# Writing out eight turns instead of one of the expert-tile loop in a mixture-of-experts stage, with the runtime-tested loop kept for what may follow

## The reference

```python
h = tok_ref(x, w1, b1, w2, b2)             # four groups mixed by softmax weights of a small MLP
h = h + attn_ref(layernorm(h), ...)        # 16 heads of 16, causal within an image
h = h + ffn_ref(layernorm(h), ...)         # shared expert and 64 routed ones, width 128
...
scores = sigmoid(logits) + gate_bias       # best 4 of 8 groups, then the best 6 experts of a token
h = silu(einsum('th,eih->eti', x, eg_w)) * einsum('th,eih->eti', x, eu_w)
routed = einsum('eti,ehi,te->th', h, ed_w, comb)
```

## Time and profile before

| what | us |
|---|---|
| median of 3 runs (lowest, highest) | 588.38 (584.45, 591.64) |
| the profiled execution's own time | 591.47 |
| its span, first to last instruction | 589.6 |
| PE busy in the span | 489.3 |
| DVE, ACT, POOL busy | 338.3, 282.3, 250.4 |

### The profile page before, as it was taken

How to read it: one execution, slowest core, us unless ns; L and a number is a source line. 1 busy time by engine, 2 the same in 40 slices (tenths; PEclk the granted TensorE clock), 3 DMA queues, 4 the chain that set the end, 5 groups by cost and what they waited for, 6 DMA issues and landing times.

```text
span 589.6 us, 12682 instructions
## 1 busy us (share of the span) xinstructions
PE 489.3 (83%) x3000; PEld 363.8 (62%) x3029; DVE 338.3 (57%) x1077; ACT 282.3 (48%) x920; POOL 250.4 (42%) x279
## 2 busy tenths in 40 slices
PE   1779898897989898767469878999998899797996
PEld 1656676675767676444148756777777687573554
DVE  4754488788888787787534333443443243332697
ACT  3394877786667676652014333444444344341100
POOL 1120115555555555567704544564564464544000
PEclk9996999999999899997679999998999899997998
DMA  8999901111111111112235467466566646542896
GB/s 277 351 321 299 252 2 55 54 56 55 56 55 55 56 55 56 54 55 99 108 100 179 127 196 220 145 198 185 152 219 189 195 125 179 164 157 80 356 387 255
DMA packets 57591, 91.05 MB, mean 154 GB/s; under 512 B 7911, under 2 KB 44650, under 8 KB 57552
## 3 DMA queue, kind: packets, MB, share of 16 engines
q1 hardware_dynamic: 44880, 62.41, 34.9%
q0 software_dynamic: 10368, 26.07, 12.3%
q10 hardware_dynamic: 2304, 2.10, 1.0%
HBM read 87.09 MB, written 41.60 MB: 218 GB/s over the span
## 4 chain that ended last, share of the span: by engine, by line
PE 31%; ACT 17%; issue 16%; DVE 11%; SPq 8%; DMA 7%; another core or an unknown queue 5%; POOL 4%; POOLq 0%; DVEq 0%; ACTq 0%
PE ps L1037 25%; ACT prob L466 8%; DMA xring<-slot_rows 3%; SPq L335 3%; SPq L340 3%; ACT kpair L480 3%; DMA y_rows<-y,xring 2%; SPq L285 2%; PE ps L1256 2%; POOL y_rows L411 2%; DVE nmax L697 2%; POOL slot_rows L380 1%; PE ps L1123 1%; ACT wring L428 1%
## 5 line engine op out<-in xcount | busy, mean ns | idle before, releaser
L411 POOL DMA_INDIRECT y_rows<-y,xring x120 | 118.1, 984 | 131.3 <-DVE y L1003 69.2
L1037 PE MATMUL ps<-wring,prob 128*128 x480 | 127.5, 389 | 11.2 <-issue 6.6
L995 DVE TENSOR_TENSOR probt<-probt,ps 128x128 f32<-128x128 f32 x120 | 34.5, 288 | 136.1 <-ACT probt L566 94.7
L1037 PEld LDWEIGHTS ps<-wring,prob 128*128 128x128 f32 x480 | 82.9, 193 | 21.5 <-issue 14.7
L561 ACT COPY prob<-ps 128x256 f32<-128x256 f32 x121 | 45.1, 374 | 67.6 <-PE ps L1256 41.2
L1037 PE MATMUL ps<-wring,probt 128*128 x240 | 74.2, 392 | 0.0
L466 ACT ACTIVATE prob<-ps,nmax 128x128 f32<-128x128 f32 x256 | 69.7, 391 | 6.3 <-DVE nmax L697 6.3
L566 ACT ACTIVATE probt<-ps 128x128 f32<-128x128 f32 x120 | 33.3, 278 | 74.6 <-PE ps L1037 46.9
L1003 DVE TENSOR_SCALAR y<-ps,xring 128x256 f32<-128x256 f32 x120 | 57.9, 483 | 12.9 <-PE ps L1037 11.2
L380 POOL DMA_INDIRECT slot_rows<-row,slot_ix x48 | 51.3, 1068 | 13.7 <-issue 13.7
L363 POOL TENSOR_SCALAR rv<-mv 128x2 f32<-128x2 f32 (+1 forms) x20 | 4.5, 222 | 123.9 <-DVE mv L890 111.9
(11 more groups left out here) (174 smaller groups left out, 792.9 us busy)
## 6 DMA issues: line engine op xcount, KB each, us to landing
wring<-wexp SPq DMA_DIRECT2D x121, 384.0 KB
xring<-slot_rows SPq DMA_DIRECT2D x121, 129.0 KB
x_sb<-y_rows SPq DMA_DIRECT2D x16, 768.0 KB, 6.7
slot_rows<-pads SPq DMA_DIRECT2D x1, 8256.0 KB, 35.7
x_sb<-x SPq DMA_DIRECT2D x3, 2048.0 KB, 17.9
slot_rows<-pads SPq DMA_DIRECT2D x5, 516.0 KB, 8.5
x_sb<-x SPq DMA_DIRECT2D x4, 512.0 KB, 5.1
out<-h_all ACTq DMA_DIRECT2D x16, 128.0 KB, 5.4
```

The costliest lines, as they stand in the source:

```text
L411: nc.gpsimd.indirect_dma_start(out=y_dram, out_offset=bass.IndirectOffsetOnAxis(ap=xring[:, q, TO_AT:TO_AT + 1].bitcast(I32), axis=0), in_ ...
L995: nc.vector.tensor_tensor(hm[:, q % 2, :], silu[:, q % 2, :], psS[q % 2][:, INTER:2 * INTER], ALU.mult).then_inc(S("h_ready"), 1)
L1037: return nc.tensor.matmul(*a, **k)
```

## The change

`FULL` = 2048 * 6 / 128 / 12 = 8 is the number of turns that every input fills. `tile_loop` now writes out these eight turns (96 tiles) on each engine, with the turn's number a constant of the program; the load of `last_turn` comes after them, and the tested loop covers turns 8 to 13. The steps, the waits, the buffers and the order of the work are the same, but where the turn's number is a constant the waits are on constants and the places in the table are fixed addresses.

```diff
+FULL = TOKENS * TOPK // P // U
...
-            for t in range(first, U):
+            for t in range(first, 0):
                 step(0, t, t, False)
-            last = eng.value_load(last_turn[0:1, 0:1], min_val=0, max_val=TURNS - 1)
-            with eng.Fori(1, TURNS) as i:
+            for i in range(FULL):
+                for q in range(U):
+                    step(i, q, U * i + q, False)
+            last = eng.value_load(last_turn[0:1, 0:1], min_val=FULL - 1, max_val=TURNS - 1)
+            with eng.Fori(FULL, TURNS) as i:
                 with eng.If(i < last + 1):
                     for q in range(U):
                         step(i, q, U * i + q, False)
```

## The result

| what | before | changed |
|---|---|---|
| median, same chip (runs; lowest, highest) | 590.01 us (4; 584.45, 596.42) | 573.94 us (4; 569.75, 575.97) |
| the profiled execution's own time | 591.47 | 569.75 |
| its span | 589.6 | 567.9 |

The ratio is 0.9748 (95% interval 0.9698 to 0.9797). By the medians that is 16.1 us, by the two profiled executions 21.7. The forecast was 20.5 us off the profiled execution's time and 567.9 for the median. The pair of traces flatters the change by 5.6 us: the one of before was above its median, the one of the changed kernel was the lowest of its four.

What follows compares the result with a forecast made beforehand. SP's sequencing was taken to bound the looped turns. Excess over PE's pace in turns 1 to 7 falls from 25.0 to 8.0 us, saving 17.0; with 3.5 from turns 8 and 9, 20.5; forecast 567.9, range 557 to 581.

Steps and rivals of the forecast that it cites:

- "All nine" waits of SP: SP's waits for PE, 3.0 us in nine cases, placed in the first turn; afterwards SP was taken as never held.
- SP's step: SP in turns 1 to 7: 1.75 us a tile falls to 1.55 (bounds 1.34 and 1.75), under PE's 1.63.
- Rival A: SP stays the bound at 1.75 us a tile in turns 1 to 7; 7 us saved, 581; chance 0.10.
- SP's waits "in nearly every tile": Sign in the changed profile: SP waits for PE (L333) in nearly every tile of the straight part instead of nine.
- PE at the turn ends: Ends of turns 0 to 6: branches go, read of three ring places stays; 1.3 us per end becomes 0.5 (bounds 0.1, 1.3).
- The loads, 3.0: Transfers where seven new experts come within nine tiles: a 3 us deficit hidden under SP's slowness appears; bounds 0 and 6.
- Rival B: Loads fill the queues: about six bursts of new experts stop PE 2 to 3 us each; 578; chance 0.07.
- Instruction fetch, 1.5: Fetching the straight code of seven turns once, about 17 more packets, costs 1.5 us in all; bounds 0 and 15.
- Rival C: Straight code starves on fetch: 17 blocks at 2 us each cost 34 us against 20.5 saved; 601.5; chance 0.06.
- Turns 8 and 9 give back 3.5: These turns stay looped, 7.8 us too long; SP enters a few tiles ahead, saving 3.5 us (bounds 0 and 5).
- The entry into the loop, at nothing: Loop entry and first load of `last_turn` move from tile 12 to 96, paid once in both; no change booked.
- The saving off the median: The 20.5 us saving, which takes the profiled 591.47 to 571.0, was subtracted from the median 588.38, giving 567.9.

Runs made afterwards that it cites:

- all but SP: PE, ACT, DVE and GpSimd write out eight turns, SP loops from turn 1; against the kernel before 0.9940 on the calm chip, 0.9916 where pauses are many.
- the second pair: Kernel before and changed kernel, both run unchanged on another chip with many pauses: 577.81 and 560.03 us, ratio 0.9697.
- the four kernels traced there: Calm chip, before 545.69 us: turns 1 to 7 written out on SP only 542.20, all except SP 541.55, PE only 540.91; changed with extra SP read 553.11.

## Why the prediction was right

- *SP is what limits the looped turns.* Shown for chips with pauses, together with the ends on PE. SP written out alone gives 8.9 to 10.5 us of some 18.5 there, leaving it in the loop leaves PE waiting for rows 12 times, and on the calm chip an extra read on SP alone makes the changed kernel slower than before.
- *"All nine" waits of SP "are in the first turn", "from then on SP is never held".* Misread. Five are in the first turn, at 311 to 317 us; the others are at 402.4, 404.2, 472.2 and 494.8, three of them behind PE's long stops at 395 and 463. They take 1.4 of the 3.0 us and leave the reading that SP limits the stage as it was, but the forecast rested its 1.55 on them. In the second trace of the same kernel SP isn't held in the first turn at all.
- *SP's step: 1.34 and a disturbance of 0.21 "that goes with GpSimd's scatters", so 1.55, "under 1.63, so SP stays ahead".* Mis-sized. SP's own step, waits taken off, is 1.66 in the first trace of the changed kernel and 1.63 to 1.71 in the other six traces with SP written out on chips with pauses. It was 1.92 before, turn ends included, and 1.83 within a turn. So the disturbance is about 0.3 on top of either code, not 0.21, and the margin under PE's pace was not there. That SP stays ahead all the same owes to the lead from the first turn and to PE's own stops, which make PE's mean 1.73: in this the forecast had luck.
- *What the disturbance is.* Half to 70% of the pauses end 1.2 to 1.4 us after a scatter's start, but on one chip the same scatters leave SP undisturbed. So the scatters alone don't make them. Rival A (the disturbance fills what was won, so nothing is won) fell: SP's own step did get shorter by 0.26. Whether the pauses grow a little where SP has room is not shown; they are 60 us in sum before and 51 after, in a stage that is itself shorter.
- *SP's waits "in nearly every tile".* Wrong as an observable, 19 cases. The right one is the lead of the row load.
- *PE at the turn ends: 1.3 now, 0.5 after.* Both hold. With SP alone written out the ends on PE are 1.3 us over pace each on the calm chip and 1.4 on the other, with the step behind each; in the changed kernel they are 3.6 us over seven, 0.5 each (4.6 and 2.1 in the other two traces). Seven ends were to save 5.6 us; all but SP saves 4.8 by the ratio on one chip and 3.3 on the calm one. What is left is seen in the changed profile ahead of the up matmuls of two of the ends (in brackets the idle time before, timeline of PE), against the 0.85 of the earlier trace rows; a third, at 348.90, has 0.92:

```profile
389.49 1.13 PE L1041 MATMUL ps<-wring,prob 128*128 x4 [0.35 <-issue]
...
429.50 1.12 PE L1041 MATMUL ps<-wring,prob 128*128 x4 [0.54 <-issue]
```

- *The loads, 3.0.* The window around the burst (345.5 to 367) has PE idle for 1.3 of 21.5 us at a share of 0.69: less than booked, and partly a turn's end. Rival B fell.
- *Instruction fetch, 1.5.* The fetch queues have, on the page of the changed kernel, against the earlier trace rows,

```profile
q8 instruction: 27, 0.44, 0.3%
q14 instruction: 34, 0.28, 0.2%
```

  9 packets more for PE (forecast 8, 26 in all) and 13 for the others (forecast 9). PE is busy in 19.50 of 19.50 us while such code streams by. Rival C, the slower side, fell: 22 packets more and the stage shorter by 20.7 us. (Its time is 567.9 + 34 = 601.9, not 601.5.) Loads and fetch together were booked with 4.5 us; 7.4 us over pace less 3.6 for the ends leaves 3.8, of which 1.4 is one stop of ACT (last section). What the fetch itself costs is not shown.
- *Turns 8 and 9 give back 3.5.* Oversized. On the first chip 2.2, on the second pair 44.3 against 44.7 from tile 95 on: nothing. They are paid in the loop as ever, and the lead with which SP enters is used up soon.
- *The entry into the loop, at nothing.* Roughly right. The end of the first turn was the entry before, 1.9 us over pace, and is 0.2 now; that end is one of the seven that the forecast counted, though it gave it the 0.8 of an ordinary one. The new entry at tile 95 is 1.5 over pace, where the ordinary end at that place was 1.6.
- *The saving off the median.* This is where the remaining distance comes from. I took 25.0 us of excess out of one execution that was itself 3.1 over its median, and subtracted the saving from the median unscaled. The second pair of traces has 158.6 - 136.9 = 21.7 us of excess in turns 1 to 7, of which 12.9 went. In the pair of traces itself the stage gave 20.7 and the whole 21.7, against 20.5 booked, so terms of the wrong size (turns 1 to 7, turns 8 and 9, what comes after tile 119) cancelled in part. By medians the change is worth 16.1, 16.7 and 18.4 us on three chips, against 20.5 forecast; the median of 573.94 lies 6.0 above 567.9 and within the range.

## What to carry to other kernels

When an engine starves periodically, compare the issuing queue's step per unit of work, turn ends and disturbances included, with the engine's own pace. Where it is longer (here 1.92 against 1.63), writing out the code of the queue's engine, with constant waits and addresses, can be worth as much as writing out the engine that seems to be the bound; here both were needed, and on the calm chip SP's part was worth the less. Judge whether a feeder is ahead by the lead of its transfers over their use, not by its waits, since it can be in time without ever being held. And a gain that rests on a disturbance is a gain of the chip it was measured on: here 2.5 to 3.3% on three chips, and on a fourth the parts gave 0.3 to 0.7%.

## What the hardware showed that I had not expected

- The same kernel of before took 590, 577, 575 and 546 us on four chips. SP's sequencer has 117 pauses in the tile stage on the first and 98 on the second (kernel of before), 96 on the third (SP alone), and 7 to 13 on the fourth (the four kernels traced there). For the changed kernel it is 94 to 111 on the three. The image stage was also shorter on the fourth chip (tile 0 at 284 to 289 us, against 299 to 309 elsewhere), so more than SP is disturbed. What in the chip makes them stays open.
- ACT stops now and then too. Its Silu starts 0.04 us after the up matmuls that it needs, in the median of every trace. In the changed kernel's first trace it once came 1.95 us late, with nothing else to do, and PE stood for what follows from it:

```profile
331.09 0.28 ACT L570 ACTIVATE probt<-ps 128x128 f32<-128x128 f32 x1 [1.85 <-PE ps L1041]
...
331.80 0.33 PE L1286 MATMUL ps<-const_sb,probt 128*128 128x128 f32 x1 [1.03 <-DVE probt L999]
```

  Stops over 1.2 us are found three times in the trace of before, once in this one, none to four times in the other eight from chips with pauses, and in none of the four from the calm chip. Most lengthen a step of PE by 1.1 to 1.6 us. The kernel of before has them as well, so written-out code isn't their cause; what is stays open.
- A turn of the loop that does nothing costs PE 0.76 us. Its compare and branch, in the changed profile, by engine (ns min/median/max):

```profile
L279 SPq COMPARE_BRANCH  x6: 14/46/50, 465.5 to 515.1; - x6
L279 PEldq COMPARE_BRANCH  x6: 83/221/352, 470.2 to 517.1; - x6
L279 ACTq COMPARE_BRANCH  x6: 45/50/699, 471.4 to 517.4; - x6
L279 DVEq COMPARE_BRANCH  x6: 61/62/63, 472.2 to 518.1; - x6
```

  PE's takes more than four times SP's. The Trainium skill, "Advanced Engine Details and Errata", section "Control Flow Timing", gives about 108 ns for a compare and branch without telling engines apart; here none has it as its median.
